# Another written-out order of the engines' work in a software-pipelined transformer layer with attention, latents and experts

## The reference

```python
ada = t_emb @ w_ada + b_ada                       # six rows of 256 per batch
xm = expmap0(layer_norm(logmap0(x)) * (1 + sc_msa) + sh_msa)
q, k, v = (to_heads(plin(xm, w, b)) for w, b in ...)       # 16 heads of 16
attn = softmax(q @ k.T / 4);  out_h = expmap0(attn @ v)
x = mobius_add(x, expmap0(g_msa * logmap0(plin(from_heads(out_h), w_o, b_o))))
xm = expmap0(layer_norm(logmap0(x)) * (1 + sc_mlp) + sh_mlp)
h = mobius_add(x, expmap0(g_mlp * logmap0(plin(plin(xm, w_f1, b_f1), w_f2, b_f2))))
local = windowed_softmax(h @ wq, h @ wk, h @ wv)           # window 64, 16 heads
remote = softmax over 64 pooled latents of h               # 8 heads
x = x0 + (gated local + gated remote) @ w_out              # x0: the input
z = x @ weight * rsqrt(sum((weight * y)**2) + 1e-8)        # y: the batch's condition
x = x + sum over the top 2 of 4 experts: w_e * relu(z @ Wi.T + (z @ A_e.T) @ B_e.T) @ Wo.T
```

## Time and profile before

| | |
|---|---|
| time, median of 3 runs | 1174.66 us (1173.78 to 1176.12) |
| the profiled execution's own time | 1173.78 us |
| its span in the profile | 1171.6 us |
| TensorE (PE) busy | 1113.9 us, 95% |
| VectorE (DVE) busy | 849.8 us, 73% |
| ScalarE (ACT) busy | 677.1 us, 58% |
| GpSimd (POOL) busy | 242.6 us, 21% |
| instructions | 32755 |

### The profile page before, as it was taken

How to read it: one execution, slowest core, us unless ns; L and a number is a source line. 1 busy time by engine, 2 the same in 40 slices (tenths; PEclk the granted TensorE clock), 3 DMA queues, 4 the chain that set the end, 5 groups by cost and what they waited for, 6 DMA issues and landing times. The chain is left out here.

```text
span 1171.6 us, 32755 instructions
## 1 busy us (share of the span) xinstructions
PE 1113.9 (95%) x13168; PEld 808.4 (69%) x13168; DVE 849.8 (73%) x3425; ACT 677.1 (58%) x1415; POOL 242.6 (21%) x336
## 2 busy tenths in 40 slices
PE   6779878999999999999999999999999999999998
PEld 3445545767677667777777677777767777777776
DVE  6899978877978786886777767867478787462443
ACT  2568757667774757476574755568374745444231
POOL 2221212041201331131303220032103120210111
PEclk9889988999999999999999999999999999999999
DMA  9310210000101001000010101000000101000000
GB/s 316 102 41 16 81 43 16 11 29 24 44 2 45 27 15 35 23 28 30 16 43 3 33 16 33 15 21 15 3 20 16 34 3 33 20 2 20 4 18 18
DMA packets 27352, 38.57 MB, mean 33 GB/s; under 512 B 3536, under 2 KB 21328, under 8 KB 27200
## 3 DMA queue, kind: packets, MB, share of 16 engines
q1 hardware_dynamic: 25296, 34.29, 9.2%
q10 hardware_dynamic: 1904, 2.20, 0.6%
HBM read 31.79 MB, written 4.29 MB: 31 GB/s over the span
## 5 line engine op out<-in xcount | busy, mean ns | idle before, releaser
L1450 ACT ACTIVATE PQ<-psq 128x2048 f32<-128x2048 f32 x112 | 209.9, 1874 | 40.5 <-PE psq L455 40.1
L1822 POOL TENSOR_TENSOR R<-R,rhoT 128x256 f32<-128x256 f32 x128 | 93.2, 748 | 452.0 <-ACT R L1450 452.0
L455 PE MATMUL psq<-QK 32*128 32x128 f32 (+5 forms) x3360 | 129.5, 305 | 0.0
L455 PE MATMUL psg<-zT,WiT 128*128 128x256 f32 x480 | 114.5, 381 | 1.1 <-DVE U L989 0.7
L455 PEld LDWEIGHTS psq<-QK 32*128 32x128 f32 (+2 forms) x3360 | 98.1, 167 | 24.5 <-issue 19.5
L455 PE MATMUL pso<-PQ,Vg 128*32 128x256 f32 (+2 forms) x2048 | 110.1, 349 | 2.5 <-ACT PQ L1450 1.8
L455 PE MATMUL psg<-WoT,R 128*128 128x256 f32 x480 | 108.9, 381 | 0.8 <-DVE R L989 0.8
L992 DVE TENSOR_REDUCE nm<-psq 128x16 f32<-128x2048 f32 (+1 forms) x48 | 92.7, 1931 | 22.3 <-PE psq L455 22.0
L1450 ACT ACTIVATE R<-psg 128x512 f32<-128x512 f32 x60 | 35.8, 596 | 114.4 <-PE psg L455 114.4
L455 PEld LDWEIGHTS psg<-WoT,R 128*128 128x128 f32 x480 | 89.2, 190 | 15.3 <-issue 2.3
L455 PEld LDWEIGHTS psg<-zT,WiT 128*128 128x128 f32 x480 | 87.0, 190 | 13.9 <-DVE U L989 1.0
(11 more groups left out here) (236 smaller groups left out, 2245.8 us busy)
## 6 DMA issues: line engine op xcount, KB each, us to landing
bcB<-ada_rows SPq DMA_DIRECT2D x16, 384.0 KB, 3.6
bcA<-ada_rows SPq DMA_DIRECT2D x15, 384.0 KB, 3.6
X<-in_x SPq DMA_DIRECT2D x16, 256.0 KB, 3.9
XR<-in_x SPq DMA_DIRECT2D x16, 256.0 KB, 2.8
out<-XR SPq DMA_DIRECT2D x15, 256.0 KB, 2.1
QK<-NMT SPq DMA_DIRECT2D x96, 4.0 KB
WiT<-in_WiT SPq DMA_DIRECT2D x1, 1024.0 KB, 5.2
WoT<-in_WoT SPq DMA_DIRECT2D x1, 1024.0 KB, 7.7
```

The source lines that it names most:

```text
L455: return e.matmul(o, lhsT, rhs, start=start, stop=stop, skip_group_check=True)
L1450: return e.activation(o, i, func, **kw)
L1822: e.tensor_tensor(R4, R4, rhoT[:, :], ALU.mult).then_inc(*pool_moe.mark(b, f"r{f}{j}"))
```

## The change

Only the strings in `ORDER` are replaced, on all five engines. Each engine's string keeps the same number of each letter, so each engine issues the same instructions, and each thread's steps keep their order; what changes is how the threads are merged. No wait is written or removed by hand; the banks of PSUM and the slots of PQ follow the new order of PE's string. The diff is one hunk, cut here to the beginning of each engine's string and the last lines of two of them (up to 33 lines per engine; each line is a piece of the string):

```diff
@@ -31,71 +31,71 @@
     "PE": [
-        "AA*n*qqqq******hh*a**a*aaaaaanooqqqqonohqhqaqqaaanaaaahqhooaqqaqaaaoaoaaNohoFhFanaaqaoaoaqqqaaoopppppphm",
-        "mohomamaaaaaNaFnFqqqqakoonkhkkkhqkwowawwowpapwpwppepemeqamNqqmFaFmaaaeeeaeeheekehekeeeeeeNkkkoFFnokwpwaw",
...
-        "kkkekewwewwewpppwemeeweemeemeemeeeeekeekekekkekwewwweweeweeeeweeeeeeeeeeeeeeeeeeeeeeeeee",
+        "A*An*qqqq******hh*a**aa*aaanaaooqqqqnoohhqqaqqaaanaaahaqhooaqqaqaaoaaoaNahooFFhanaaqoaaoaaqqaqoopppppphh",
+        "mmoommaaaaaaNnaFFqqqqakoonkkhhkkqkwowawwopwppwpawpepemeqqmqaNmFmeaaFeaehaeeaeehkeenkeeeeeeNkFkFkookwpwaw",
...
+        "kkkekewwewwewpppwemewemeemeemeeeeeekeeekekekkekwewwweweeweeweeeeeeeeeeeeeeeeeeeeeeeeeeee",
     ],
     "DVE": [
-        "ssssPPPPPPPPPP*PPPPPPPPPPPPPPPPPPPPPPPPPPPPPPPPPAAAssnnnnnsnssssnsPPsPqqPPqqPqPPPPPsPPqsPqqqqPPqPsqPqPPq",
-        "qPhPhPhsPsPPsPPs*PP*PsPPsPP*Ps*PshsPPsPP*sPPs*sPP*******P*s*s*sPPPnPPPPPPPnPnPnoonoonPonoqoqoPoPoPooqPoq",
-        "oqoooqqPqqPqPqPqnqqnqnhhnPnohonPPPnhPPqffPfPfPfPPqfPfPfPfPfPfPfPfPffqfqffqffqqfqnfnqfnfqqqnfqnfqfffqfPhP",
-        "nPPPhnhPPhPPPPPqPooPPPoPPooPPoPoPPoqoPoPPoPoPPoPPqPoPoqqPPPoPPPoPqPqqPPqqqqqqqoohhfooNfNofhNoNffNffNfNoo",
-        "fFoFFFfFofofFfohfofFofFFFfffFfFnFnfFfnfonFnofononoqfgggfggggfgoogggfgfgqfggfgfgggggfgfgfgqgqqgfofoqffqfq",
-        "ofqfofqfoffopfqofoqfqofffqoqfofohfhfhfopfsffPsPhPmPoPPoPoPoPPPsPPmPPPoPoPmPpfPPfPPfPfPfPfPPfPfPfPfPPffPf",
...
-        "eeeeeweeeeeepmeweemememeeeeeeeeeeeeeeeeeeeeeeepwewwwewewwwwweeeweeeeeeeeeeeeeeeeeeeeeeeeeeeeeeee",
+        "*ssssPPPPPPPPPPPPPPPPPPPPPPPPPPPPPPPPPPPPPPPPPPPAssssnnnnnnnAAssssPPsPsPsPqPsqPsPsPsPqqqPssPsPsqPsqPsqPs",
+        "qPsqPsqPqPqPqPqPhhhhPPPP*P*P*P*PPPPPPPPPPPPPPs*Ps*P*P*s*Ps*nP*nP*nP*nP*nP*o*onPonPooqoqoPoPoPoPoPqoqoqoP",
+        "oPoPoqPnqPnqPnqPnqPnqPnqPnqPqPqPhhhhooPPPPPPPPffPqfPqfPfPfPfffffffqfqfqfffffqfnqfnqfnqfnqnqnqnqfqfqfhfff",
+        "PPPPPhPhPhPPPqPPoPoPoPoPoPPoPoPoPqPoPoPoPoPoPqPoPqPoPoqPoPPPPPPPqPqPqPqPqqqqqqoohNNNfNfNhNfhNfhfofofofoF",
+        "fFfFfoFfnFfnFoFnoFnoFnoFfnFfnFfoFfoFfoFfofofofofofqggfgfgfgfgfgfggggogogggggfgfgqggfgfgfgfqgfqgfqfofofof",
+        "qpfqfofqfofqfqfqfsfqfofqfoqsoqohhhhpfpfofofsfofmPoPsoPoPoPoPPPPPmPPPPPPPoPoPPPmPfmPfPfPfPfPfPfPfPfPfPfPf",
...
+        "eeepepeeeeeeeeeemwmememeeeeeeeeeeeeeeeeeeeeeeeeeeewwwwwwwwwweeweeeeeeeeeeeeeeeeeeeeeeeeeeeeeeeee",
     ],
     "ACT": [
-        "PnnnnnqqP**hh*aan*aananna*nooqnnPqnnonhffhffaqfnnaqnnaffaanahhooPaqanqaoNaNaNffaNNffhnoohafnnnaggffgogaa",
-        "ffgaffqggaqpfooppfpfpphohfffPfafaNNnaaNnNNnnfnfaqnnqaknggoNkggonkhnkgkNhkogNwgafpfffpwNfpapffeeppeeeNqqa",
...
+        "Pnnnnnqq*P*hh*a**annannaanaooqPnnnqnnohffhffaqfnnanqnanffaahahooPaqannqaoNNaaNNffNfafhoohnnafnagggfgfoaa",
+        "gffaffqggaqpfopopffppphhoPffffafannNNffaNNannNnaNNqnnaqknngngkggookhhkkgNNkoggawpffffppwpfaffpeepeePqeNq",
...
     ],
     "POOL": [
-        "nnnn****nnnnnnnnffnnnnNNNNffnnnnggffffNNnNNnnnnnnnggNNNNffeeeegeegenNnneNNNnggNNNNffnnnnggeeffeeeeeennnn",
...
+        "nnnn****nnnnnnnnffnnnnNNNNffnnnnggffffnnNNNNnnnnnnggNNNNffeennnneeggeeNeeNNNggNNNNffnnnnggeeffeeeeeennnn",
...
     ],
     "SP": [
-        "Axxn*x*wAxA*nNnnw*n*nx*NnmNxmnNxNnexmwxnemNNwnmxNenwemNwxnmNxnewmewNnmNewnmewNmewNmNewmNewmewmewmewee",
+        "nwxxwxx*****AAAnNn*nnNnxnmNxnmNewxNnmxNnmexwNnmNexwnmewxNnNmexwnmewNnmNewnmewNmewNmewNmNewmewmewmewee",
     ],
```

More of the change, by code:

```diff
@@ new lines @@
+        "gggNgNgNgNgNgNgNgggeeFFFFoFoFoFoFoFowFowFowpwFowFowFwowFoososswsowogoggggggggggggwgpgpNoNoNgNgNgNgNgffqg",
+        "fgfgfgmfqfgfgfqmfqfFfFmfqfmfqfqfFfqfFfqfFqfFqfFqfpqFnqFfqfhfFnfFnfFnfFnsFnsFnsshhhggqggegegegegqegegegeg",
+        "egqegegegegegegegegeoeoeoegoeoegogwowogwowowogwowowoooowweoofpfpffffffffffffmwfeffffffffmfefqffmfeffPPPP",
+        "PPPmPPPPPPPPPPPPPPPPeeqPPPPPPqPqPqPqPqPqpqPqPqPqPhPsPsPsPsPhhhnnnnnnnNNNNNNNqFFoFoFoFoFoFFFoFoFoFoFoFoFo",
+        "eoeoeoeoeoqggwqwgegegegqwgewgewgewgwgwgoNgoNgeNwNgwNgNfNgfgefgefgefgpgfpgfegfefefewgfegmfeFfeFfeFfmfqfFf",
@@ new lines @@
+        "FmfqfefqfqmfqfeqfqfqfqfefqFfqFnhFnFnFneFnFnFnFFgggggggggggeeggggghhhpgggggggogooosssoosgogooooooooooooff",
+        "qfffffffffffffwfwffefefwfewfewfewfewewefefwfwfqfefePePeqpPepPePePePePePePePePePPPPPqPPPPPwPPPPPmPqPPPPPP",
+        "qmPqPePqPqmPqPePqmPqPqeqqhneNnNnNnNnNnNnNeehhhFFoFoFoFoFoFFFoFoFoFoFoFoFoqoposossogosggggggggggggggggoog",
+        "NgNgNgNgNfNfNgfgfffffgwfwfgfwfewfewfefefefFfefefefFwfewfewfeFeFeFweFwfqfeFfefFefqfeFweFeFeFeFpeFpFgggqgg",
+        "megggggmeggqggmqeqnqmqeqngqngqngqngqngqnghhhhggggggeeoooooooopooooosossosooooffwfwffefefwfewfewfewfewfew",
@@ new lines @@
+        "feeewewfefefqfefefefefefefepfepefefffffPPPPPPPPPPPPPwPPPPmqPPPPPPqPmePPqPPmePPPPmPPqPePqPqPqPqPqPqPqPqqq",
+        "heNNNNNnNnNnnnnneehhhFFoFoFoFoFoFFFoFoFoFoFoFoFoqoqogqpogqqogogggqgqgqgqgqgqgqgqNqNqNhNgNgNgNgoogggggwfw",
+        "fwfewfewfegfewfewfewfegfefefefegwfwfegfefefenfefnefnefnefnefneneeffffpfpfwmeFmememFeFFFFFFFFFFFFFggggggg",
+        "ggggeeggghhhpgogogogoggggggoogogooooooooooqooffffffqffffffqwfwfewfewfewfefefefwfewfewfefeeeeqfwfwfeqfefe",
+        "fpepeqeqeqePqePqePqPqPqPqPqwhPmPPPPPPPPPPPmePPpmePPPPPPmPePPPPPPPPPPePPPPPeeNNNNNNNhhhnnnnnnnFFoFoFoFoFo",
@@ new lines @@
+        "FFFoFoFoFoFoFoFooooooggqggoogggNgNgNwNwNfNfNgfwfgwfgwfgwfgwfgwfgfgfgfgefgegegefqefgefgefefeqwefweqefgefg",
+        "efefefeepepefwefefefffpmmqqmeqqqmqqeqqqqheeeehhhoooooooooooooooooFooeefefeFefFefFwefwefFefFefFefwefwefwe",
+        "fwefwewefFefFefFefFefFwefwefFfFfFfpfpfgfffffPgPmwPePgPgPgPgPgPgPmPePgPgPmPePgPgPgPmPgPgePgPgPgPgPgPgPgPg",
+        "PgPPPPgPgPPPPPPPPeeNNNNNNNpoooooFoooFoFoFoFoFoFoFoFoFoFFFFFggggoogggggffegegfegfegfefefefefgefwNfwNfeNfg",
+        "NwNfwNfwNfwfewfewfewfewfegfefgefgegepepfegfegfegfgfgfPwgPgPmFPPFPFPFPFPFPFPFPFPFmeFPFpmeFPFmFPPePgPPPPgP",
@@ new lines @@
+        "eaaeaehnnNNegnngagehgkenkgNNggNkkkNNookpawgpggpwpgaogpNNNffpffggqfnnqannpnaffeepahpggkheegkgaeqkgkkeookg",
+        "egaweoaffppffpwefeeffPqapeeaapnnhNNnpnknhNNeNekaoNNokkkggegqgokawNNgaffNpffwppggefenneqnnneffeaaeahggggg",
+        "apkhooggkppkokffeefkfeefkweffapqppewaPeqeeeannNNeaahnnNNnNahoNNokeepggkggppokgkNNffNkffeegkgfewaffpwqapp",
+        "eeggaeggeaenngqnenanahhggkoeoepkeepkokffkfpfkweafppffpewaPeqeeeqaaennNNahNNnnNahoNNoneekggpqkggnnqkkoNNk",
+        "eegffkNffaewggfpnpnpnaffewpaepeeeaeagggghgpakhooggpkpeeokffkffkeeqkfaewffppqawpeeePepeaeannNNNNnahnNnakh",
@@ L90 @@
+        "oNNokpggpkgkoeekgNNffNkffeegafweqggapwpffppeppeqeeaeaeaheeakhookeekokffkffekawfeaeppgffpggewgeePegaggNNa",
+        "NaNNeeapkookNNeeggopggkffkffkNpgNkNefwpepffwpggeeepegPpgggepkgNNkNgNgNkkkeekeewepwpeepggeggepeepgggkkeep",
+        "kkkeekewppwepeepeepepkkkkkkeeeewepppeweeeeekeekeekekkekeweeweeeeeeeeeeeee",
     ],
     "POOL": [
[L92 to L93 removed]
```

55 lines of the change are left out of this document (14 added, 41 removed).

## The result

The changed kernel takes 1182.32 us in the median of 4 runs (1181.61 to 1183.55), the kernel before 1174.22 (1171.65 to 1176.12). The ratio is 1.007, with a 95% interval of 1.0054 to 1.0087: 8.1 us slower, and 1.3 us above the upper end of the range that was given. The profiled execution of the changed kernel has a span of 1179.4 us, 7.8 more than before.

What follows compares the result with a forecast made beforehand. Loads, then DVE bound the opening, TensorE from 210 us; time is TensorE's fixed work plus idle. -1.3 - 2.0 - 1.0 = -4.3 us from 1173.78 gives 1169.5, with 0.88 to the median 1170.4 us; range 1163 to 1181.

Steps and rivals of the forecast that it cites:

- The opening: Run to 150 us: -1.3 us to 60 us (ends -3 and +3.5) and -2.0 us from 60 to 150 us.
- U<-U,hf: DVE's product of batch 0, before at 33.42 us: 3.0 to 3.5 us later, behind statistics of batches 4 to 6.
- the scores: TensorE's scores of batch 0, before at 37.76 us: start near 41 us, a loss that comes back later.
- the wait for lq: TensorE's 2.74 us wait for the small table lq in the opening goes, as a value product now stands ahead.
- Norm(1): DVE's first step of norm(1), now before the Bst casts, waits for ACT's JA: some 2.3 us of new DVE idle.
- the gain of 2 us in VectorE's stretch: 60 to 150 us, where DVE is 94% busy and TensorE waits for it: -2.0 us, ends -4 and 0.
- The -1.0 us for 150 to 210 us: DVE's 4.91 us idle filled, fewer like neighbours, one ACT exponential 1.8 us later: -1.0 us, ends -3 and +2.
- SyncE's string at nothing: SyncE's opening: condition-row stores moved behind loads and weights, some 9 us of cover before bcA's reader, so no cost.
- The interleaving's price: DVE's short steps: each pair of neighbours of one stage costs 0.11 us more than an alternating pair.
- The step that failed: 210 to 1100 us: TensorE 99% busy, so DVE's saved 13 us is worth 0, ends -4 and +6.
- The forecast of VectorE's busy time: Whole run, named as a sign that the prediction is right: DVE's total busy time falls below 849.8 us.
- rival 3: Middle loses: steps placed too early block engines, TensorE's idle in 890 us goes 8.3 to some 18; 1181 us, chance 0.14.

Runs made afterwards that it cites:

- experiment 1: New order up to 150, 250 or 700 us, old behind: 0.998, 0.9985, 1.0035 of before; new throughout 1.007; old to 250 us, then new: 1.0127.

## Why the prediction was wrong

**What held.** The opening: the prediction took -3.3 us to 150 us, and the new order to 150 us measures -2.3 us. Within it single terms were off and evened out. U<-U,hf came 1.2 us later, not 3.0 to 3.5; the scores came at 38.77 us, not 41; the wait for lq went as forecast; nmr was ready at 43.74, not 45; ScalarE's third exponential and OT came 2.3 and 2.8 us before the forecast times. Norm(1) cost 0.53 us of idle DVE, not 2.3. The stores of the condition's rows issued at 32.64 us, not 29.4, and bcA at 38.19 (near 39). Against that, TensorE now waits 3.71 us for batch 2's M at 63 us, in the place of its wait for OS, and the gain of 2 us in VectorE's stretch didn't come: the step at 150.66 us is 2.5 us early, less than the 4.2 us at OT. That the sum to 150 us came out within 1 us is thus partly luck: a gain larger than forecast in the first stretch made up for one that didn't come in the next. The -1.0 us for 150 to 210 us didn't come either: the lead is 2.5 us at 150.66 us and 2.5 at w_out's first step. SyncE's string at nothing: shown, with the other strings as before. The interleaving's price, forecast at 0.11 us for an equal pair, measured 0.064 to 0.085.

**The step that failed** is "DVE loses 123 like neighbours and 13 us of its time, and this is worth nothing: TensorE is 99% busy. What could move is the 8.3 us of waits: I take 0, with ends -4 and +6", for 210 to 1100 us, and ahead of it the sentence on which it rests, that "TensorE's work (fixed, but for its clock) plus this idle time" is the time. The lead of 2.3 us became a lag of 8.2 us: the work behind 150 us costs 10.5 us, uncertain by 2.6 us. TensorE's idle time from 300 to 1100 us grew only from 7.6 to 10.9 us (800 less busy time in the earlier trace rows and after), and by under 1 us more in the other stretches behind 150 us. The granted clock there is 1.00 both times, and higher than before from 150 to 210 us. So some 6 us lie in time that counts as busy, of which the sum had no term. What the runs put in its place:

- TensorE's own work isn't fixed. Each change between strip and full-width products costs 0.205 us where TensorE runs them alone, 0.08 to 0.10 us by the rows of this kernel, and 0.09 to 0.12 us where changes were added to it. The new string has 38 more, 34 of them behind 150 us: about 3 us. That they exist and cost is shown; a changed kernel with these 34 taken out again was not run.
- TensorE's waits grew, by some 4 us of visible idle time. Late PSUM banks may be a part of them, since the order of TensorE's string also hands out the banks: 1.9 us by the times (3.5 less the 1.6 that the kernel before gains by a list made in the same way), which isn't clear of nothing.

That leaves some 3 us of the 10.5 open. Short waits for inputs or banks may be in it: a record of a matmul ends later than the next one starts (427.00 + 1.89 = 428.89, the next at 428.73), so a wait shorter than this overlap leaves no idle time in the page. No run here measures them. The changes can't be the whole, by their places too: the kernels of experiment 1 have 376 (new order to 150 us), 406 (to 700) and 410 (throughout). From 150 to 700 us, 30 more changes go with 6.4 us; from 700 us on, 4 more go with 4.1 us.

**The forecast of VectorE's busy time** was wrong too: it rose from 849.8 to 862.7 us. The records themselves grew, before and after:

```profile
L986 DVE TENSOR_TENSOR sf<-sf 128x2 f32<-128x2 f32 x192 | 32.4, 169 | 9.5 <-ACT sf L1450 6.8
L1005 DVE CUSTOM_DVE_ANT_0 JD<-X,UO 128x256 bf16<-128x256 f32 x32 | 15.9, 514 | 9.2 <-POOL UO L1812 9.2
```

```profile
L986 DVE TENSOR_TENSOR sf<-sf 128x2 f32<-128x2 f32 x192 | 39.4, 206 | 5.1 <-ACT sf L1450 2.8
L1005 DVE CUSTOM_DVE_ANT_0 JD<-X,UO 128x256 bf16<-128x256 f32 x32 | 20.4, 651 | 7.0 <-POOL UO L1812 7.0
```

The same 192 small steps take 206 ns in the mean instead of 169, the same 32 wide ones 651 instead of 514. As in the earlier trace rows, where a record of 0.17 us is followed after 0.08 us, an instruction's record here can begin while the one before it still runs; that the longer records come from this was not tested by itself. Busy time of VectorE is no measure of its work here.

**The rivals.** The outcome is nearest to rival 3, "the middle loses", at 1181 us: right in its place and in its size (+10 less the opening's gain), and only in part in its mechanism: it put the 10 us into idle time, which it had grow from 8.3 to 18 us in 890 us and which grew to 11.4. So its size is in part luck. It had 0.14. What spoke against it, "DVE is 72% and ACT 59% busy there, so most blocks are absorbed", is contradicted by the run with grouped chains in the middle: 27.9 us.

## What to carry to other kernels

Where a bound engine runs at 99%, ask two things before a new order is costed at nothing: whether its own work depends on what stands next to what (on TensorE, products on strips beside full-width ones), and which resources are handed out in its order. Count work done in a stretch (the number in brackets), not busy time, to see whether an engine keeps its pace. Written-out orders for several engines are one object: a piece from the start can be taken over (0.998), TensorE's string without the others', or theirs without it, can't (1.24 and 1.19); and choosing banks by release instead of in turn is a small gain that adds no instruction (0.9986 on the kernel before; on top of the new opening its 0.9 us is within the noise).

## What the runs showed of the hardware that was not expected

- TensorE alternating between steps of products on 32-partition strips and steps on 128 partitions, nothing to wait for: 3.00 us a pair; in blocks of eight 2.64 us. It shows as 100% busy at full clock both times.
- In the changed kernel's trace a full-width step of 8 products takes 1.73 us among its like and 1.83 us right behind a strip step, with no idle time shown, while a score step takes 1.07 to 1.08 us with full-width steps or values beside it.
- VectorE: in the order with more alternation the same instructions are recorded as longer (169 to 206 ns, 514 to 651 ns), and yet undoing part of the alternation made the kernel slower, by 0.064 to 0.085 us for each equal pair.
